# Filler rows, scatters, weight split and final gates of a mixture-of-experts block, rearranged around its drain

## The chip, the cores and the metric

The kernel runs on one core of a Trainium2 chip. The time is device microseconds of one execution. Engines are named as in the profile: PE (TensorE), DVE (VectorE), ACT (ScalarE), POOL (GpSimd) and SP (SyncE, which here only starts transfers). The kernel before has a median of 1559.16 us over three runs.

## The reference

The block takes 32 batches of 256 rows of 128 numbers. It is an attention layer followed by a mixture-of-experts feed-forward layer, each with a gate and a residual sum:

```python
mod = (_silu(L0_c) @ L0_wmod).reshape(L0_c.shape[0], 6, 1, -1)
sa, ca, ga, sb, cb, gb = (mod[:, k] for k in range(6))      # ga, gb are then kept at least 0.25 from zero
h = _layernorm(x) * (1 + ca) + sa
x = x + ga * attention(h)
h = _layernorm(x) * (1 + cb) + sb
x = x + gb * feed_forward(h)

# feed_forward: a router picks 2 of 8 experts for each row
logits = h @ router_w.T + router_b
topv, topi = top_k(logits, 2); gates = softmax(topv)
for e in range(8):
    w = sum(gates * (topi == e))
    y = (silu(h @ gate_w[e].T) * (h @ up_w[e].T)) @ down_w[e].T     # 128 -> 512 -> 128
    out += y * w
```

Everything is float32. The attention has 16 heads, each the difference of two softmaxes, and is not touched.

## The kernel before

The program has three stages. There is no scheduler: each engine's instructions stand in the order of the code, and engines wait for each other through semaphores.

**Attention, rounds.** `iterations` runs rounds i = -4 to 34. In one round eight batches are in work, each at another step: batch i (`b2`) has its scores, i-1 (`bC`) is normalised, i-2 (`bW`) gets its output product and residual sum, i-3 (`bR`) is routed. A round has 16 sub-steps `s`. The last three rounds, 32, 33 and 34, have no scores left; they are called the drain here. In them, for `bW`: DVE makes `on_tok` (L1308, s = 0), PE transposes it (L927), ACT copies it, PE multiplies by `wo` (L939), DVE makes `xtmp` (L1318), POOL adds it to `xres` (L1453), DVE takes statistics and inverse roots (L1267 to L1284), ACT writes the normalised row into `h2` (L1117). For `bR`: POOL scales and shifts `h2` in two passes (L1460 at s = 0, L1464 at s = 2), PE transposes it (L955) and multiplies by the router (L961), DVE picks the experts and counts (L1347 to L1402); `carry` holds the next free place of each expert, `idx` the place of each row. POOL then scatters the batch's four pieces of 128 rows into `rows_sorted` in DRAM (L1482, s = 12 to 15). `rows_sorted` has a region for each expert, and each row carries 128 numbers, the number of its place in `pair_out` and its gate.

**The way to the tiles.** An expert's rows seldom fill its last tile of 256, so filler rows (place number out of bounds, so never stored) are written behind each expert's end: `ffn_sp` reads the end from `endi` and starts one transfer per expert (L464 to L466), 256 rows each and 2304 behind the last. DVE makes tables of 72 tiles: each tile's expert (`tile_exp`) and first row (`tile_row`), L605 to L625. SP waits for the tables, the filler and all scatters, and then loads tile 0 (L482).

**Weights in two parts.** PE multiplies in a rounded float32 form, so a weight is used as a high part and a low part. `split_weights` (L389 to L402) does this on DVE for two experts in each of the three drain rounds and for two more behind the tables: for each half of an expert's weights a copy, a difference and a copy in place, so that `w_hi` holds the high and `kt`'s storage the low parts. For each tile ACT then copies the expert's high part into `w_now` (`bring_high`, L557) and DVE the low part (`bring_low`, L636).

**Feed-forward, tiles.** 72 tiles of 256 rows. For tile j PE transposes the rows of j+1 (L526), computes gate and up in two halves of three passes each (L515), and the down product of j-1 (L545). DVE splits the rows (L644, L646) and multiplies the halves (L654), ACT applies SiLU (L570) and scales the result (L579), POOL scatters it into `pair_out` (L680).

**Final sum.** 16 groups of two batches, in a ring of four slots. SP loads both experts' results (L498, two transfers) and the gates `gb`, repeated over the partitions, from DRAM (L501, one transfer); DVE adds the two results (L667) and multiplies by the gates (L670), POOL adds `xres` (L693), and a transfer started by ACT stores the group.

Of the kernel before, what the change touches and what calls it, by code (L numbers as in the profile page):

```python
# [5 lines left out]
F32 = mybir.dt.float32  # L6
F32R = mybir.dt.float32r
# [7 lines left out]
P = 128  # L15
# [30 lines left out]
LAST_PADS = FFN_TILES - ROUTED // FT + 1  # L46
# [53 lines left out]
def adaln_block(nc, x, w_qk, w_v, w_o, lambdas, rms_col, router_w, router_b, gate_w, up_w, down_w,  # L100
                c_t, w_mod, max_ones, ident, mask_q, before, iota, ramp, pair_no, tile_no, filler, out):
    ctx = ExitStack()
    with ctx:
# [50 lines left out]
        w_hi = sb("w_hi", [P, 2, NE * FF])  # L154
        wg, wu = (w_hi[:, k, :] for k in range(2))
# [146 lines left out]
        w_split = sem("w_split")  # L302
# [16 lines left out]
        fin_step = sem("fin_step")  # L319
        fin_done = sem("fin_done")  # L320
# [58 lines left out]
        lo_weights = kt[:].rearrange("p a t h k -> p (a t h k)").bitcast(F32)  # L379
        w_lo = lo_weights.rearrange("p (j k) -> p j k", j=2)  # L380
        wg_lo, wu_lo = (w_lo[:, k, :] for k in range(2))
# [8 lines left out]
        def split_weights(dve, c):  # L390

            V = nc.vector
            for w, lo in ((wg, wg_lo), (wu, wu_lo)):
                at = slice(c * FF, (c + 1) * FF)
                V.tensor_copy(lo[:, at].bitcast(F32R), w[:, at]).then_inc(w_split, 1)
                split_steps[0] += 1
                dve.wait_ge(w_split, split_steps[0])
                V.tensor_tensor(lo[:, at].bitcast(F32R), w[:, at], lo[:, at], ALU.subtract).then_inc(w_split, 1)  # L398
                split_steps[0] += 1
                dve.wait_ge(w_split, split_steps[0])  # L400
                V.tensor_copy(w[:, at].bitcast(F32R), w[:, at]).then_inc(w_split, 1)
                split_steps[0] += 1  # L402

        split_steps = [0]
        SPLIT_STEPS = 2 * 3 * NE
# [9 lines left out]
        fin_gb = (pair_view[:, FIN_RING * NF:FIN_RING * (NF + GROUP * DIM)]  # L415
                  .rearrange("p (a b c) -> p a b c", a=FIN_RING, b=GROUP))
# [41 lines left out]
        TABLE_STEPS = 17  # L458
# [1087 lines left out]
```

## Time and profile before

| | us |
|---|---|
| three runs | 1559.16, 1554.7, 1559.51 |
| the profiled execution | 1545.11 |
| its span, first to last instruction | 1543.4 |

Over the span PE is busy 1307.1 us (85%), DVE 1136.2, ACT 957.8 and POOL 875.8. The mean granted TensorE clock is 0.953 of full speed. The profile splits the span in 40 slices, and PE's digits are 9 nearly everywhere, except at the start, in four slices from the 27th on (the drain) and in the last two (the final sum). A busy share over the whole span mixes the stages, so the tables by stretch of time are read instead. The chain of work that ended last is followed back by the profile from the last instruction, each piece to what released it.

### The profile page before, as it was taken

Reading aid. Unit: us, or ns where it says so; the run is one execution under the profiler, and the core shown is the slowest. Engines: PE = TensorE matmul, PEld = TensorE weight load, DVE = VectorE, ACT = ScalarE, POOL = GpSimd, SP = SyncE. Lnnn points to the kernel's source line nnn. Section 1 sums busy time; section 2 is a strip of 40 time slices with the busy share of each in tenths; the row PEclk is TensorE's granted clock in tenths of the full one; section 3 lists DMA queues with packets and bytes.
Section 4 is the critical chain, followed back from the end, with each engine's and each line's share of the span. In section 5 each row is a group of like instructions: output and inputs, shape, how many; then the busy total and the mean of one; then the engine's idle time right before and its main releaser. Section 6 shows DMA issues by size and latency. Waiting matters only on the chain. (4 is left out here: it accounts for less than half of the span.)

```text
span 1543.4 us, 41532 instructions
## 1 busy us (share of the span) xinstructions
PE 1307.1 (85%) x13658; PEld 1068.2 (69%) x13785; DVE 1136.2 (74%) x2899; ACT 957.8 (62%) x2007; POOL 875.8 (57%) x1287
## 2 busy tenths in 40 slices
PE   1589999999999999999999999984179999999940
PEld 0366777767777777677776777663179999999940
DVE  4567888888888888888888888877745555555535
ACT  1166777777777777777777777763145555555520
POOL 2134667676777777677677677775313433444434
PEclk9999999999999999999999999996579999999985
DMA  6443345344434443444344434410121111111239
GB/s 218 119 110 84 107 119 127 91 113 121 124 93 121 114 124 91 121 120 118 91 127 113 120 92 117 118 39 22 46 71 52 53 51 52 52 55 52 54 103 283
DMA packets 178897, 154.20 MB, mean 100 GB/s; under 512 B 20851, under 2 KB 161401, under 8 KB 178340
## 3 DMA queue, kind: packets, MB, share of 16 engines
q1 hardware_dynamic: 161144, 124.63, 31.5%
q0 software_dynamic: 8704, 16.93, 3.6%
q10 hardware_dynamic: 8880, 10.49, 1.9%
q8 instruction: 93, 1.52, 0.4%
q14 instruction: 76, 0.62, 0.1%
HBM read 89.87 MB, written 63.14 MB: 99 GB/s over the span
## 5 line engine op out<-in xcount | busy, mean ns | idle before, releaser
L1021 ACT ACTIVATE probs<-p_exp 128x512 f32<-128x512 f32 x768 | 446.6, 602 | 176.1 <-PE p_exp L845 158.0
L1435 POOL TENSOR_SCALAR_AFFINE_SELECT probs<-probs 128x256 f32<-128x256 f32 (+1 forms) x768 | 365.5, 485 | 283.3 <-ACT probs L1021 275.5
L1199 DVE TENSOR_REDUCE mx<-p_max 128x2 f32<-128x512 f32 x512 | 351.2, 687 | 154.6 <-PE p_max L819 153.8
L680 POOL DMA_INDIRECT pair_out<-probs,v x144 | 141.5, 983 | 233.8 <-ACT probs L579 207.0
L817 PE MATMUL p_max<-kt,qt 96*128 96x256 bf16 x1024 | 198.6, 275 | 46.2 <-DVE mx L1199 24.4
L868 PE MATMUL p_out<-probs,v 128*32 128x256 f32 (+1 forms) x4096 | 220.8, 333 | 15.0 <-POOL probs L1435 8.7
L845 PE MATMUL p_exp<-qt,kt 100*128 100x256 bf16 x1024 | 196.0, 273 | 17.5 <-DMA qt<-max_parts 17.3
L1202 DVE TENSOR_REDUCE mx<-p_max 128x4 f32<-128x512 f32 x256 | 173.0, 676 | 1.6 <-PE p_max L828 1.6
L868 PEld LDWEIGHTS p_out<-probs,v 128*32 128x32 f32 x4096 | 112.3, 109 | 86.0 <-POOL probs L1435 25.1
L1482 POOL DMA_INDIRECT rows_sorted<-h,idx x128 | 136.7, 1068 | 51.1 <-issue 19.4
L817 PEld LDWEIGHTS p_max<-kt,qt 96*128 96x128 bf16 x1024 | 89.2, 101 | 90.1 <-DVE mx L1199 25.5
L570 ACT ACTIVATE ot<-p_exp 128x512 f32<-128x512 f32 x144 | 86.1, 598 | 90.9 <-PE p_exp L515 85.8
L819 PE MATMUL p_max<-mask,idb 128*128 128x256 bf16 x512 | 140.7, 275 | 0.0
L515 PE MATMUL p_exp<-rows_hi,w_now 128*128 128x256 f32 x576 | 140.0, 305 | 0.6 <-DVE w_now L636 0.6
L515 PE MATMUL p_max<-rows_hi,w_now 128*128 128x256 f32 x576 | 127.5, 283 | 0.0
L845 PEld LDWEIGHTS p_exp<-qt,kt 100*128 100x128 bf16 x1024 | 98.1, 98 | 37.5 <-DMA qt<-max_parts 23.7
L1011 ACT ACTIVATE ot<-p_out,out_scale 128x256 f32<-128x256 f32 x256 | 106.6, 472 | 0.0
L851 PE MATMUL p_exp<-qt,kt 100*128 100x128 bf16 x1024 | 99.4, 219 | 7.1
L1441 POOL TENSOR_TENSOR part_l<-rest,part_m 128x512 bf16<-128x512 f32 x64 | 74.4, 1162 | 52.0 <-ACT part_m L1037 52.0
L825 PE MATMUL p_max<-kt,qt 96*128 96x128 bf16 x1024 | 100.8, 221 | 2.0 <-DVE mx L1199 1.1
L515 PEld LDWEIGHTS p_exp<-rows_hi,w_now 128*128 128x128 f32 x576 | 100.0, 191 | 1.0 <-issue 1.0
L851 PEld LDWEIGHTS p_exp<-qt,kt 100*128 100x128 bf16 x1024 | 79.4, 98 | 30.5 <-issue 0.6
(166 smaller groups left out, 2770.6 us busy)
## 6 DMA issues: line engine op xcount, KB each, us to landing
qt<-q_parts SPq DMA_DIRECT2D x64, 384.0 KB
q_parts<-part_h SPq DMA_DIRECT2D x96, 128.0 KB, 2.0
kt<-k_parts SPq DMA_DIRECT2D x128, 96.0 KB
v<-rows_sorted SPq DMA_DIRECT2D x72, 130.0 KB, 2.2
q_parts<-part_m SPq DMA_DIRECT2D x64, 128.0 KB, 2.0
kt<-k_parts SPq DMA_DIRECT2D x128, 64.0 KB
qt<-pair_out SPq DMA_DIRECT2D x32, 256.0 KB, 5.2
mods<-mod_rows SPq DMA_DIRECT2D x32, 192.0 KB, 3.9
```

The costliest lines, as they stand in the source:

```text
L515: m = nc.tensor.matmul(to[:, f * FT:(f + 1) * FT], w_now[:, par, w, kind, (f0 + f) * P:(f0 + f + 1) * P], rows[:, par, :], start=(k == 0), ...
L680: nc.gpsimd.indirect_dma_start(pair_out, bass.IndirectOffsetOnAxis(rows_in[:, j.slot, t, DIM:DIM + 1].bitcast(U32), 0), rows_out[:, j.slot ...
L817: nc.tensor.matmul(p_max[:, bank, t * SEQ:(t + 1) * SEQ], qt[0:QK_ROWS, slot, h8, P:SEQ], kt[0:QK_ROWS, slot, t, h8, :], start=(t == 0), s ...
L819: m = nc.tensor.matmul(p_max[:, bank, :].rearrange("p (t k) -> p t k", t=2)[:, :, P:SEQ], idb[:], mask4[:, 0:2, :], start=False, stop=True)
L845: m = nc.tensor.matmul(p_exp[:, bank, t * SEQ:(t + 1) * SEQ], kt[0:ALL_ROWS, slot, t, h8, 0:P], qt[0:ALL_ROWS, slot, h8, :], start=True, s ...
L851: m = nc.tensor.matmul(p_exp[:, bank, c:c + P], kt[0:ALL_ROWS, slot, t, h8 - 1 + hh, P:SEQ], qt[0:ALL_ROWS, slot, h8 - 1 + hh, P:SEQ], sta ...
L868: m = nc.tensor.matmul(p_out[32 * j:32 * j + 32, g % 2, SEQ - n:SEQ], v[:, b.par, tile, 2 * g + j // 2, :], src, start=(tile == 0), stop=( ...
L1021: nc.scalar.activation(probs[:, g % 2, k, :], p_exp[:, k, :], ACT.Exp, scale=SCALE).then_inc(exp_done.sem, 1)
L1199: m = V.reduce_max(mx[:, w, 1, :, h8:h8 + 1].rearrange("p t o -> p (t o)"), p_max[:, bank, :].rearrange("p (t k) -> p t k", t=2), AX.X, ne ...
L1202: m = V.reduce_max(mx[:, w, 0, :, h8 - 1:h8 + 1], p_max[:, bank, :].rearrange("p (t h k) -> p t h k", t=2, h=2), AX.X, negate=True)
L1435: G.affine_select(out=blocks, in_=blocks, compare_op=ALU.is_ge, fill=zero, base=0, pattern=[[0, 2 if k < 2 else 4], [1, P]], channel_multi ...
L1482: G.indirect_dma_start(rows_sorted, bass.IndirectOffsetOnAxis(idx[:, bR.par, k:k + 1].bitcast(U32), 0), h2[:, bR.par, k // NT, k % NT, :], ...
```

## The change

1. *Filler.* `endi` is now copied one batch earlier, when the last batch but one (30) has been routed, and 512 rows are written behind each expert's end as it stands then (`AHEAD`), which covers what the last batch can add. The 2048 rows behind the eight regions have a fixed place and are written at the start, by a transfer that ACT issues. POOL's first scatter of the last batch waits for all nine.
2. *Scatters.* Batch 30's four scatters move from s = 12 to 15 of round 33 to s = 3 to 6 of round 34.
3. *Weights.* `split_weights` is gone. The weights stay whole in `w_all`; ACT's copy into `w_now` rounds them as before, and DVE makes the low part of a tile's expert as `w_all` less that copy, for which it waits for the copy.
4. *Tables.* Tiles behind the last expert's are told by an eighth comparison, since they lie in the fixed filler.
5. *Final gates.* The repeated gates come from PE: a column of the identity, repeated, times `mrow`, into four PSUM banks. The transfer from `mod_rows` is gone.

```diff
-LAST_PADS = FFN_TILES - ROUTED // FT + 1
+LAST_PADS = FFN_TILES - ROUTED // FT
+AHEAD = (SEQ + FT) // P
+FILLS = NE + 1
...
-        def split_weights(dve, c):
...
-                V.tensor_copy(lo[:, at].bitcast(F32R), w[:, at]).then_inc(w_split, 1)
...
-                V.tensor_tensor(lo[:, at].bitcast(F32R), w[:, at], lo[:, at], ALU.subtract).then_inc(w_split, 1)
...
-                V.tensor_copy(w[:, at].bitcast(F32R), w[:, at]).then_inc(w_split, 1)
...
-        fin_gb = (pair_view[:, FIN_RING * NF:FIN_RING * (NF + GROUP * DIM)]
-                  .rearrange("p (a b c) -> p a b c", a=FIN_RING, b=GROUP))
+        fin_gb = (p_exp[:, 0, :], p_exp[:, 1, :], p_max[:, 0, :], p_max[:, 1, :])
...
-                start = sp.value_load(endi[0:1, e:e + 1], min_val=0, max_val=SORTED_ROWS - LAST_PADS * FT)
-                pads = (FT if e < NE - 1 else LAST_PADS * FT) // P
-                sp.dma_start(rows_sorted[bass.ds(start, pads * P), :].rearrange("(m p) r -> p m r", p=P),
-                             fill[:].unsqueeze(1).to_broadcast([P, pads, RW])).then_inc(filled, 16)
+                start = sp.value_load(endi[0:1, e:e + 1], min_val=0, max_val=NE * REGION - AHEAD * P)
+                sp.dma_start(rows_sorted[bass.ds(start, AHEAD * P), :].rearrange("(m p) r -> p m r", p=P),
+                             fill[:].unsqueeze(1).to_broadcast([P, AHEAD, RW])).then_inc(filled, 16)
...
-                sp.dma_start(fin_gb[:, g.slot, :, :],
-                             mod_rows[bass.ds(g.n * GROUP, GROUP), 3 * DIM:4 * DIM].unsqueeze(0)
-                             .to_broadcast([P, GROUP, DIM])).then_inc(fin_loaded[g.slot], 16)
...
-            pe.wait_ge(w_split, SPLIT_STEPS)
...
+            pe.wait_ge(hid_ready, 2 * FFN_TILES)
+            for g in range(NB // GROUP):
+                if g >= FIN_RING:
+                    pe.wait_ge(fin_step, 2 * (g - FIN_RING) + 2)
+                for j in range(GROUP):
+                    b = g * GROUP + j
+                    m = nc.tensor.matmul(fin_gb[g % FIN_RING][:, j * DIM:(j + 1) * DIM],
+                                         idf[0:NB, b:b + 1].to_broadcast([NB, P]), mrow[:, 3, :], start=True, stop=True)
+                m.then_inc(gb_ps, 1)
...
-                    V.tensor_copy(w_now[:, j.c % 2, 1, :, :], w_lo[:, :, bass.ds(w0, FF)]).then_inc(low_here, 1)
+                    t_wait(dve, high_here, j)
+                    V.tensor_tensor(w_now[:, j.c % 2, 1, :, :], w_all[:, :, bass.ds(w0, FF)],
+                                    w_now[:, j.c % 2, 0, :, :].bitcast(F32), ALU.subtract).then_inc(low_here, 1)
...
+                dve.wait_ge(gb_ps, g.n + 1)
                 fo = fin_out[:, g.slot, :].rearrange("p (b t c) -> p b t c", b=GROUP, c=DIM)
-                V.tensor_tensor(fo, fo, fin_gb[:, g.slot, :, :].unsqueeze(2).to_broadcast([P, GROUP, NT, DIM]), ALU.mult).then_inc(fin_step, 1)
+                gb = fin_gb[g.slot][:, 0:GROUP * DIM].rearrange("p (b c) -> p b c", b=GROUP)
+                V.tensor_tensor(fo, fo, gb.unsqueeze(2).to_broadcast([P, GROUP, NT, DIM]), ALU.mult).then_inc(fin_step, 1)
...
             act.wait_ge(setup_v, SETUP_DONE)
+            act.dma_start(rows_sorted[NE * REGION:SORTED_ROWS, :].rearrange("(m p) r -> p m r", p=P),
+                          fill[:].unsqueeze(1).to_broadcast([P, LAST_PADS * FT // P, RW])).then_inc(filled, 16)
...
-                    for c in range(2):
-                        split_weights(dve, 2 * (i.c - NB) + c)
...
                             V.tensor_copy(idx[:, bR.par, :], posf[:]).then_inc(route.sem, 1)
+                            if bR.c == NB - 2:
+                                V.tensor_copy(endi[:], carry[:]).then_inc(tables, 1)
...
+            def scatter(b, k):
+                if k == 0:
+                    wait(pool, route, b, ROUTE_ROWS)
+                    wait(pool, h2_copied, b)
+                    if b.c == NB - 1:
+                        pool.wait_ge(filled, 16 * FILLS)
...
-                    if s in (12, 13, 14, 15) and active(bR):
...
+                    if s in (12, 13, 14, 15) and active(bR) and bR.c != NB - 2:
+                        scatter(bR, s - 12)
+                    if s in (3, 4, 5, 6) and bR.c == NB - 1:
+                        scatter(bR.plus(-1), s - 3)
```

How the order of the instructions moves is shown at three places. The first is DVE at the start of round 33, before the change: the roots of round 32 (`rstd`, `neg_mr`), the first split group (one half of one expert), of which three more alike follow, and then `on_tok`.

```order
L1282 SCALAR_TENSOR_TENSOR rstd<-nt,root 128x36
L1284 SCALAR_TENSOR_TENSOR neg_mr<-mvs,rstd 128x4
L395 CAST kt<-w_hi 128x512
L398 TENSOR_TENSOR kt<-w_hi,kt 128x512
L401 CAST w_hi<-w_hi 128x512
```

From the same list, the end of the fourth group and what follows it: `on_tok` stands behind all twelve.

```order
L398 TENSOR_TENSOR kt<-w_hi,kt 128x512
L401 CAST w_hi<-w_hi 128x512
L1308 TENSOR_TENSOR on_tok<-o,rstd 128x512
L1318 TENSOR_TENSOR xtmp<-p_mix,mods 128x256
L1242 BN_STATS stats<-xres 128x6 x2
```

The same place after the change, with that program's own line numbers (L1289 is `on_tok`, L1299 `xtmp`).

```order
L1270 SCALAR_TENSOR_TENSOR rstd<-nt,root 128x36
L1272 SCALAR_TENSOR_TENSOR neg_mr<-mvs,rstd 128x4
L1289 TENSOR_TENSOR on_tok<-o,rstd 128x512
L1299 TENSOR_TENSOR xtmp<-p_mix,mods 128x256
L1230 BN_STATS stats<-xres 128x6 x2
```

Twelve instructions between the roots and `on_tok` are gone; the same holds for rounds 32 and 34, and behind the tables.

The second place is POOL from the end of round 32 to the first stores of the tiles, before the change; each row of four DMAs is one batch's scatters (29, 30, 31), `h<-h,mods` are the two passes.

```order
L1482 DMA rows_sorted<-h,idx 69888x130 x4
L1460 TENSOR_TENSOR h<-h,mods 128x2x128
L1464 TENSOR_TENSOR h<-h,mods 128x2x128
L1453 TENSOR_TENSOR xres<-xres,xtmp 128x256
L1482 DMA rows_sorted<-h,idx 69888x130 x4
L1460 TENSOR_TENSOR h<-h,mods 128x2x128
L1464 TENSOR_TENSOR h<-h,mods 128x2x128
L1482 DMA rows_sorted<-h,idx 69888x130 x4
L680 DMA pair_out<-probs,v 16384x128 x12
```

And after it, where the eight DMAs are batch 30's and batch 31's scatters.

```order
L1428 DMA rows_sorted<-h,idx 69632x130 x4
L1453 TENSOR_TENSOR h<-h,mods 128x2x128
L1457 TENSOR_TENSOR h<-h,mods 128x2x128
L1446 TENSOR_TENSOR xres<-xres,xtmp 128x256
L1453 TENSOR_TENSOR h<-h,mods 128x2x128
L1457 TENSOR_TENSOR h<-h,mods 128x2x128
L1428 DMA rows_sorted<-h,idx 69632x130 x8
L666 DMA pair_out<-probs,v 16384x128 x12
```

Batch 30's scatters have gone behind the passes over batch 31's `h`; batch 29's still stand ahead of those over batch 30's.

The third place is SP from the last tile's load (`v<-rows_sorted`) to the loads of the first two groups of the final sum, before the change.

```order
L482 DMA v<-rows_sorted 128x2x130
L498 DMA qt<-pair_out 128x4x128 x2
L501 DMA probs<-mod_rows 128x2x128
L498 DMA qt<-pair_out 128x4x128 x2
L501 DMA probs<-mod_rows 128x2x128
```

And after it; the last row is the eight loads of the first four groups.

```order
L461 TENSOR_LOAD tile_row
L461 ISA x2
L462 ISA
L462 DMA v<-rows_sorted 128x2x130
L478 DMA qt<-pair_out 128x4x128 x8
```

Of three transfers a group two are left.

## Rows read from the trace of the kernel before

**Rows 1.** Windows: length; busy (x) PE, PEld, DVE, ACT, POOL; clock; DMA share; GB/s.

```profile
1050.00:1130.00 80.00, 19.49 (x130) 13.93 (x129) 50.46 (x161) 15.17 (x38) 29.65 (x32) 0.54 0.17 48
1130.00:1480.00 350.00, 349.37 (x2988) 349.00 (x2988) 202.31 (x357) 203.44 (x354) 137.56 (x140) 0.99 0.19 51
1480.00:1543.40 63.40, 4.41 (x37) 4.01 (x35) 30.86 (x33) 1.85 (x5) 24.49 (x21) 0.58 0.83 232
```

**Rows 2.** Timeline of PE in the drain: start, duration, what, [idle before <-releaser].

```profile
1063.72 1.09 PE L927 MATMUL p_mix<-idf,on_tok 128*128 128x128 f32 x4 [2.92 <-DVE on_tok L1308]
...
1089.24 0.69 PE L955 MATMUL p_mix<-idf,h 128*128 128x128 f32 x2 [0.52 <-DVE xtmp L1318]
```

**Rows 3.** Timeline of DVE in the drain.

```profile
1054.31 0.42 DVE L395 CAST kt<-w_hi 128x512 fp32r<-128x512 f32 x1
...
1076.59 0.42 DVE L395 CAST kt<-w_hi 128x512 fp32r<-128x512 f32 x1
...
1083.51 1.17 DVE L1308 TENSOR_TENSOR on_tok<-o,rstd 128x512 f32<-128x512 f32 x1
...
1113.63 0.23 DVE L625 SCALAR_TENSOR_TENSOR tile_row<-tileno,qt 128x72 int32<-128x72 f32 x1
```

**Rows 4.** Timeline of POOL in the drain.

```profile
1076.74 1.15 POOL L1482 DMA_INDIRECT rows_sorted<-h,idx  x1 [3.40 <-DVE idx L1402]
...
1082.15 1.15 POOL L1460 TENSOR_TENSOR h<-h,mods 128x256 f32<-128x256 f32 x1
1083.38 0.75 POOL L1464 TENSOR_TENSOR h<-h,mods 128x256 f32<-128x256 f32 x1
...
1112.89 0.96 POOL L1482 DMA_INDIRECT rows_sorted<-h,idx  x1 [0.30 <-issue]
```

**Rows 5.** Timeline of ACT in round 33.

```profile
1095.56 0.88 ACT L1117 ACTIVATE h<-xres,neg_mr,rstd 128x128 f32<-128x128 f32 x2 [1.55 <-DVE neg_mr L1284]
```

**Rows 6.** The chain that ended last, in order of time: start, duration, what.

```profile
1101.17 0.70 POOL h L1460
...
1102.84 0.67 PE p_mix L955 x2
...
1108.08 0.15 DVE idx L1402
...
1109.39 0.41 SPq L466
...
1117.46 7.54 DMA rows_sorted<-fill
...
1125.78 2.17 DMA v<-rows_sorted
```

**Rows 7.** DMA issues: what, queue, count, size of each, median us to landing.

```profile
pair_out<-probs,v POOLq DMA_INDIRECT x144, 2.3
...
rows_sorted<-fill SPq DMA_DIRECT2D x7, 130.0 KB, 2.3
```

**Rows 8.** Windows, columns as in rows 1: the filler's transfer, and the final sum.

```profile
1122.00:1123.00 1.00, 0.00 (x0) 0.00 (x0) 0.00 (x0) 0.98 (x2) 0.00 (x0) 0.50 1.21 253
1530.00:1535.00 5.00, 0.00 (x0) 0.00 (x0) 3.81 (x5) 0.00 (x0) 2.52 (x2) 0.50 1.16 338
```

**Rows 9.** Timeline of DVE in the final sum: the first and the last group's add.

```profile
1495.90 0.69 DVE L667 TENSOR_TENSOR probs<-qt 128x512 f32<-128x512 f32 x1 [12.76 <-DMA probs<-mod_rows]
...
1536.05 1.55 DVE L667 TENSOR_TENSOR probs<-qt 128x512 f32<-128x512 f32 x1 [0.43 <-DMA probs<-mod_rows]
```

**Rows 10.** Timeline of one DVE instruction of the setup, and of a tile.

```profile
26.45 1.23 DVE L1188 TENSOR_TENSOR probs<-probs,idf 128x1024 f32<-128x1024 f32 x1
...
1308.72 1.05 ACT L557 CAST w_now<-w_hi 128x1024 fp32r x1 [0.20 <-PE p_max L515]
1309.46 0.69 DVE L636 CAST w_now<-kt 128x1024 fp32r x1 [0.16 <-issue]
...
1311.69 0.37 PE L515 MATMUL p_exp<-rows_hi,w_now 128*128 128x256 f32 x1
```

More of the change, by code:

```diff
@@ L153, in adaln_block @@
         mrow = sb("mrow", [NB, 4, DIM])
-        w_hi = sb("w_hi", [P, 2, NE * FF])
-        wg, wu = (w_hi[:, k, :] for k in range(2))
+        w_all = sb("w_all", [P, 2, NE * FF])
         wd = sb("wd", [P, NE * FF])
@@ L556, in bring_high @@
                     w0 = act.value_load(tile_exp[0:1, bass.ds(j.n, 1)], min_val=0, max_val=(NE - 1) * FF)
-                    nc.scalar.copy(w_now[:, j.c % 2, 0, :, :], w_hi[:, :, bass.ds(w0, FF)]).then_inc(high_here, 1)
-            act.wait_ge(w_split, SPLIT_STEPS)
+                    nc.scalar.copy(w_now[:, j.c % 2, 0, :, :], w_all[:, :, bass.ds(w0, FF)]).then_inc(high_here, 1)
+            act.wait_ge(ffn_w_loaded, 48)
             act.wait_ge(tables, TABLE_STEPS)
@@ L595, in ffn_vector @@
             V = nc.vector
-            count = [0]
+            count = [1]
             def step(ins):
@@ L603, in ffn_vector @@
             dve.wait_ge(route.sem, ROUTE_STEPS * NB)
-            step(V.tensor_copy(endi[:], carry[:]))
             step(V.tensor_tensor(ends[:], carry[:], posm_ramp[:], ALU.subtract))
@@ L612, in ffn_vector @@
             step(V.tensor_scalar(jump[:], first[:], -float(FT), float(REGION), ALU.mult, ALU.add))
[L613 removed]
+            for e in range(1, NE):
                 step(V.tensor_tensor(first[:, e:e + 1], first[:, e:e + 1], first[:, e - 1:e], ALU.add))
[L616 removed]
+            ge = table_view[:, 0:FFN_TILES * NE].rearrange("p (j e) -> p j e", e=NE)
             sums = table_view[:, FFN_TILES * NE:FFN_TILES * (NE + 1)]
             dve.wait_ge(pv_done.sem, PAIRS * NB)
[L619 to L620 removed]
+            step(V.tensor_tensor(ge, tileno[:].unsqueeze(2).to_broadcast([P, FFN_TILES, NE]),
+                                 first[:].unsqueeze(1).to_broadcast([P, FFN_TILES, NE]), ALU.is_ge))
             step(V.reduce_sum(sums, ge, AX.X))
[L622 to L623 removed]
+            V.tensor_scalar(tile_exp[:], sums, float(FF), float((NE - 1) * FF), ALU.mult, ALU.min)
+            step(V.tensor_tensor(ge, ge, jump[:].unsqueeze(1).to_broadcast([P, FFN_TILES, NE]), ALU.mult))
             step(V.reduce_sum(sums, ge, AX.X))
@@ L626, in ffn_vector @@
             assert count[0] == TABLE_STEPS, count
-            for c in range(2 * TAIL, NE):
-                split_weights(dve, c)
-            assert split_steps[0] == SPLIT_STEPS
+            dve.wait_ge(ffn_w_loaded, 48)
             def bring_low(j):
@@ L661, in final @@
             def final(g):
-                dve.wait_ge(fin_loaded[g.slot], 48 * (g.turn + 1))
+                dve.wait_ge(fin_loaded[g.slot], 32 * (g.turn + 1))
                 if not g.static:
```

43 lines of the change are left out of this document (8 added, 35 removed).

## The prediction

> **What bounds the kernel now.** I read the windows by stage first. In the feed-forward tiles PE is busy for 349.37 of 350.00 us at a granted clock of 0.99 [rows 1]: nothing off PE's path is worth anything there, and whatever makes PE wait is paid 72 times. Between attention and the tiles (1050 to 1130 us, the drain) no engine is full: PE is busy 19.49 of 80 us and the DMA share is 0.17 [rows 1]. That is a chain of single steps, and a step taken out of it is worth its full length. In the final sum PE is all but idle and the DMA share is 0.83 over the stretch [rows 1] and 1.16 in the middle of it [rows 8]: the transfers look like the limit. The change touches all three.
>
> Which steps of the drain count I read from the timelines of PE, DVE and POOL beside each other and from the chain of waits. The drain has three rounds (32, 33, 34). In round 32 PE has ended its last `p_out` work and sits idle for 2.92 us, until 1063.72, for `on_tok` [rows 2], while DVE splits weights from 1054.31 on [rows 3]. In round 33 the split runs from 1076.59 to 1083.51 [rows 3]; POOL meanwhile issues four scatters, from 1076.74 to 1082.15, and then makes its two passes over `h`, the second until 1084.13 [rows 4]. In round 34 `h` is ready for POOL at 1096.44 [rows 5], but POOL comes to it at 1101.17, behind four more scatters [rows 6]. After the last `idx` (1108.23) come eight issues of filler from 1109.39 on; the last starts at 1117.46 and takes 7.54 us to land, and only then does the first tile's load start, at 1125.78 [rows 6].
>
> **The change part by part.** All times are on the clock of the profiled execution.
>
> *Split out of round 32.* Twelve instructions leave DVE, but PE has other work until 1063.72 - 2.92 = 1060.80 [rows 2], so 2.9 us come back. If POOL's masks and scatters, which release that other work, also ran quicker without the split beside them, it could be up to 2 us more; I take none of it.
>
> *Split out of round 33.* DVE's branch would bring PE's transposes of `h` (1089.24 [rows 2]) forward by 6.9 us [rows 3]. But they also need POOL's second pass, which as it is ends at 1084.13 [rows 4]; PE would start some 0.15 later, at 1084.3: 4.9 us. So POOL is late next. Its own pace: a scatter beside the split took 1.15 us, the very last one, after the split group beside it began but among nothing else of POOL's, 0.96 [rows 4]; if all four come down to 0.96, 0.8 us more. I take a little over half, 5.4 us. The Trainium skill, page "SBUF — State Buffer", section "Who interferes with whom", says that VectorE's copies and casts in a two-port mode lock GpSimd out of the shared ports, through which it writes its descriptors. By that rule in full the round gives 5.7 us back, without it 4.9; the trace has both durations, but a split runs beside the short one too, so it bears the rule out only in part.
>
> *Scatters moved behind the passes over `h`.* In round 34 POOL can start on `h` at 1096.5 [rows 5] in place of 1101.17 [rows 6], 4.7 us, less some 0.2 for the `endi` cast that now stands ahead of the roots on DVE: 4.5 us. The four scatters are not gone: they stand between these passes and the last batch's scatters. The next `idx` comes 5.4 us after PE's transposes start (1102.84 to 1108.23 [rows 6]); four scatters of 0.96 us with gaps of 0.30 [rows 4] and 0.7 us ahead of them are 5.7. Nearly hidden, and the filler (below) is later anyway.
> So far 2.9 + 5.4 + 4.5 = 12.8 us: the last `idx` at 1095.4.
>
> *Filler ahead.* The eight issues now follow the last batch but one. Its `idx` comes 5.4 us after its transposes, at 1094.65 (1089.24 + 5.4), less 2.9 + 5.4 = 8.3 us: 1086.35. The first issue follows `idx` by 1.15 us as now (1108.23 to 1109.39, `endi` cast included), so 1087.5; the eighth 8.1 us later (1109.39 to 1117.46 [rows 6]): 1095.6. It carries 260 KB. The 130 KB ones landed in 2.3 us [rows 7], the 1170 KB one in 7.54 [rows 6]; on that line 3.0. All eight are 2.13 MB in 8.1 us, 263 GB/s, and the big one ran at 253 GB/s with the engines full [rows 8], so they queue a little: I take 3.8 us, landed at 1099.4 (bounds 1098 to 1103). This is a new wait. The last batch's first scatter stands behind it on POOL, behind that the other three, and SP waits for all of them before it loads tile 0. From 1099.4: 0.3 us, 3 x 1.27 to the start of the fourth scatter, 2.3 us to land (as the tiles' scatters do [rows 7]): 1105.8. SP then takes 0.8 us, as between the filler's landing (1125.02) and the load (1125.78) [rows 6]: the load starts at 1106.6 in place of 1125.78, 19.2 us earlier. The tables need 1113.86 - 1108.23 = 5.6 us from `idx` [rows 3, 6], now some 0.4 more (one more step, 576 elements for 504): 1101.4, in time. The split's last group behind them was hidden under the filler already.
>
> *Low part made per tile.* DVE's copy of 128x1024 takes 0.69 us; a TENSOR_TENSOR of 128x1024 took 1.23 [rows 10]. Before the first tile this is on the path: 0.5 us. In the loop it must also wait for ACT's high copy, which ends at 1308.72 + 1.05 = 1309.77 [rows 10]; so the low part runs from 1309.9 to 1311.1, and PE takes up the next tile's weights at 1311.69 [rows 10]. A margin of 0.5 us: cost 0. Here the change could lose most.
>
> *Final sum.* Group to group it takes (1536.05 - 1495.90) / 15 = 2.68 us [rows 9]. A group moves 512 KB in, 256 KB out and 128 KB of gates (896 KB). With the engines at 1.16 [rows 8] I let time follow bytes: 2.68 x 128 / 896 = 0.38 us a group, 5.7 us over 15, and 0.3 for the issue that goes ahead of the first group's data: 6.0 us. Bounds: 0, if the ring of four slots sets the pace and not the bytes; 9, if the landing gets quicker on top. DVE's multiply now reads PSUM, which no row shows in this stage; I bound it by the add of its shape, 0.69 alone and 1.55 beside POOL's add [rows 9], at 0.69. PE's gate products are due long before they are read.
>
> *Start.* ACT issues 1.06 MB of filler behind 6 MB of weights. At 253 GB/s [rows 8] that is 4.2 us of the engines, at worst all on the path, at best none. I take 0.3 us, near the lower end, since nothing waits for this filler before the drain. The Trainium skill, "DMA: Bandwidth & Descriptors", section "Issuing engines are not separate DMA queues", speaks against the change here: DMAs of ACT, SP and GpSimd run on the same 16 engines and interleave. If the first batches' loads stood behind it in full, the sum would be 20.5 in place of 24.4 us; the trace of before has no such transfer.
>
> **Sum**: 19.2 - 0.5 + 6.0 - 0.3 = 24.4 us. The profiled execution would go from 1545.11 us (span 1543.4) to 1520.7. The median of the runs, 1559.16, lies 14 us above the profiled execution, and nothing in the trace says why; taken off the median: 1534.8 us.
>
> **Rivals.**
> (a) The final sum gives nothing: its pace is the ring. From the fifth group on a slot's loads wait for POOL's sum in that slot; SP's issues, landing, DVE's two steps and POOL's add are 4 x 2.68 us around. For: DVE's add grows from 0.69 to 1.55 us beside POOL's add [rows 9], and both stay. Against: the share of 1.16 [rows 8], and that one of the issues in this very ring goes. Gain 18.4: 1540.8. Chance 0.14.
> (b) The filler lands late. If the transfers and POOL's scatters jam the engines so that the last lands as late as the 1170 KB one did, 7.5 us after its issue [rows 6], 3.7 us go, and with them the 0.5 of POOL's own pace and part of the final sum. Gain 19 or less: 1541. Chance 0.10.
> (c) More than forecast: round 32 gives 2 more, the filler isn't late at all (3 more), the final sum 9 in place of 6. Gain 32: 1527. Chance 0.12.
> (d) Slower than before: the low part makes PE wait in every tile. A TENSOR_TENSOR of two SBUF inputs grew from 0.69 to 1.55 us beside POOL [rows 9]; were the low part stretched alike, 1.23 x 1.55 / 0.69 = 2.8 us, PE would wait 2.8 - 1.23 - 0.5 = 1.0 us a tile, 74 us over 72 tiles: 1609. It decides from 24.4 / 72 = 0.34 us of wait a tile on, a low part of 2.1 us. Against: in the tiles POOL has scatters and no adds, and between its two of a tile and the next two lies the time of the low part. The SBUF page's same section lets two SBUF inputs contend only with a GpSimd instruction that reads SBUF. Chance 0.04, a quarter of it small enough to end within 0.3%.
> (e) The change does nothing: the drain ends in another wait as long, such as tile 0 on its tables and on ACT's first high copy. The tables are there at 1101.4 and the copy takes 1.05 us [rows 10], long before the rows: too early to decide. Chance 0.02.
>
> **How the numbers follow.** Forecast 0.58, (a) 0.14, (b) 0.10, (c) 0.12, (d) 0.04, (e) 0.02. The range takes in (a), (b) and most of (c), and goes a little further down than their sum because the base is loose: the runs before spread from 1554.7 to 1559.51 with the profiled one at 1545.11. 1522 to 1545. About 0.3% (4.7 us) is what a measurement of this kernel can tell from no change. Faster 0.94 (forecast, (a), (b), (c)), same 0.03, slower 0.03.
>
> **What would show it.** Right: no cast into `kt` in the drain; PE's transposes of `on_tok` straight behind its `p_out` work; POOL's passes over `h` straight behind ACT; the last batch's first scatter released by a filler DMA; tile 0's load 19 us earlier; the tiles at the pace of before with DVE's low part at 1.23; groups of 2.3 us in the final sum. Wrong: PE waiting for `w_now` in the loop, groups still at 2.7 us, or the last batch's first scatter more than 5 us behind `idx`.

## The result, and the profile after

The changed kernel took 1537.6 us (median of four runs, 1527.53 to 1540.76) against 1556.93 for the kernel before (median of four, 1553.02 to 1559.51): a ratio of 0.9864, 95% interval 0.9836 to 0.9893, which is 21.2 us less (17 to 26); the two medians as they stand are 19.3 us apart. The forecast was 1534.8 us, 24.4 less than the 1559.16 us that the kernel before had then; one more run has since moved that median to 1556.93, so the time came a little closer to the forecast than the gain did.

The two profiled executions are 1543.4 us of span before and 1538.6 after, only 4.8 apart. That is no contradiction. The attention stage, which the change leaves alone, is not equally long in every execution: PE's last `p_out` work ended at 1060.80 in the profile before and at 1077.17 in the one after, and over the ten profiles of this study, all with the same code for the attention rounds, it ended anywhere from 1060.57 to 1077.17. So I set all clocks to zero at the end of PE's last `p_out` work and compare from there. On that clock the rest takes 482.60 us before (1543.4 - 1060.80) and 461.43 after: 21.2 us, which fits the timed ratio. The forecast column splits the prediction's 19.2 us up to the load of tile 0 into the pieces that it names and a rest.

| piece, from trace to trace | before | after | gained | forecast |
|---|---|---|---|---|
| round 32: last `p_out` to the end of its roots (`neg_mr`) | 15.87 | 12.90 | 2.97 | 2.9 |
| round 33: to PE's transposes of batch 30's `h` | 12.57 | 6.92 | 5.65 | 5.4 |
| round 34: to those of batch 31's `h` | 13.60 | 8.90 | 4.70 | 4.5 |
| from there to the load of tile 0 | 22.94 | 21.69 | 1.25 | 6.4 |
| to the first product of tile 0 | 5.32 | 6.10 | -0.78 | -0.5 |
| the tiles, to the last down product | 354.23 | 354.57 | -0.34 | 0 |
| final sum, to POOL's last add | 54.43 | 46.80 | 7.63 | 6.0 |
| last store | 3.64 | 3.55 | 0.09 | 0 |

PE in the drain of the changed kernel (timeline: start, duration, what, idle before and its releaser). L913 transposes `on_tok`, L941 transposes `h`.

```profile
1075.66 1.51 PE L854 MATMUL p_out<-probs,v 128*32 128x256 f32 x16 [3.68 <-POOL probs L1418]
1077.10 1.12 PE L913 MATMUL p_mix<-idf,on_tok 128*128 128x128 f32 x4
...
1096.99 0.66 PE L941 MATMUL p_mix<-idf,h 128*128 128x128 f32 x2 [2.25 <-POOL h L1457]
...
1105.89 0.66 PE L941 MATMUL p_mix<-idf,h 128*128 128x128 f32 x2 [4.46 <-POOL h L1457]
```

The 2.92 us of idle time before the `on_tok` transposes [rows 2] are gone, and PE now waits for POOL in round 33, as forecast. POOL, from the end of round 33:

```profile
1104.30 0.68 POOL L1453 TENSOR_TENSOR h<-h,mods 128x256 f32<-128x256 f32 x1 [6.78 <-ACT h L1105]
1105.06 0.68 POOL L1457 TENSOR_TENSOR h<-h,mods 128x256 f32<-128x256 f32 x1
1105.89 1.01 POOL L1428 DMA_INDIRECT rows_sorted<-h,idx  x1 [0.15 <-issue]
...
1109.74 0.96 POOL L1428 DMA_INDIRECT rows_sorted<-h,idx  x1 [0.30 <-issue]
1120.65 0.96 POOL L1428 DMA_INDIRECT rows_sorted<-h,idx  x1 [9.95 <-DMA rows_sorted<-fill]
```

The passes over `h` start right behind ACT's row, in place of behind four scatters [rows 4 to 6]. But the last batch's first scatter then waits 9.95 us for the filler. The chain of waits of the same stretch, in order of time:

```profile
1102.28 0.18 DVE endi L1385
...
1103.41 0.41 SPq L446
...
1112.56 7.20 DMA rows_sorted<-fill
...
1124.44 2.27 DMA rows_sorted<-h,idx
...
1127.58 2.31 DMA v<-rows_sorted
```

The path now runs from batch 30's `endi` through the eight transfers to the last batch's scatters. Round 34, with the gain of 4.7 us in it, lies beside this path and not on it. The engines behind the filler (windows: length, busy time of PE, PEld, DVE, ACT, POOL, clock, DMA share, GB/s):

```profile
1108.00:1110.00 2.00, 0.10 (x1) 0.00 (x0) 1.35 (x10) 0.48 (x2) 1.39 (x3) 0.50 1.24 164
1110.00:1112.00 2.00, 0.25 (x4) 0.19 (x4) 1.48 (x13) 0.00 (x0) 0.70 (x1) 0.50 1.30 178
1112.00:1114.00 2.00, 0.00 (x0) 0.00 (x0) 1.69 (x10) 0.00 (x0) 0.00 (x0) 0.50 1.19 176
```

They are full at 164 to 178 GB/s, where the one long transfer before moved 253 at the same share [rows 8]. Neither rate is steady. The first four microseconds of the eight transfers moved more, at a lower share:

```profile
1104.00:1106.00 2.00, 0.11 (x1) 0.14 (x2) 0.00 (x0) 0.22 (x1) 1.47 (x3) 0.50 0.66 200
1106.00:1108.00 2.00, 1.45 (x6) 1.07 (x6) 0.00 (x0) 0.68 (x2) 1.70 (x2) 0.50 0.84 237
```

And the long transfer of the kernel before, in the three microseconds ahead of the one in [rows 8]:

```profile
1119.00:1120.00 1.00, 0.00 (x0) 0.00 (x0) 0.97 (x2) 0.00 (x0) 0.00 (x0) 0.50 0.95 295
1120.00:1121.00 1.00, 0.00 (x0) 0.00 (x0) 0.08 (x1) 0.00 (x0) 0.00 (x0) 0.50 1.03 287
1121.00:1122.00 1.00, 0.00 (x0) 0.00 (x0) 0.00 (x0) 0.44 (x1) 0.00 (x0) 0.50 1.20 189
```

With the 253 of [rows 8] its four microseconds average 256 GB/s.

In the tiles, PE stays busy for 349.37 of 350 us, to the hundredth what it was [rows 1]; the low part takes 1.23 us and ends 0.57 us before PE's first product of the next tile:

```profile
1134.00:1484.00 350.00, 349.37 (x2995) 349.16 (x2995) 238.96 (x355) 204.11 (x355) 138.46 (x140) 1.00 0.19 50
```

```profile
1311.64 1.05 ACT L543 CAST w_now<-w_all 128x1024 fp32r x1 [0.19 <-issue]
1312.81 1.23 DVE L619 TENSOR_TENSOR w_now<-w_all,w_now 128x1024 fp32r<-128x1024 f32 x1 [0.60 <-ACT w_now L543]
...
1314.61 0.37 PE L491 MATMUL p_exp<-rows_hi,w_now 128*128 128x256 f32 x1
```

In the final sum DVE's first and last add, against those of [rows 9]:

```profile
1497.40 0.69 DVE L651 TENSOR_TENSOR probs<-qt 128x512 f32<-128x512 f32 x1 [11.35 <-DMA qt<-pair_out]
...
1532.02 0.68 DVE L651 TENSOR_TENSOR probs<-qt 128x512 f32<-128x512 f32 x1
```

(1532.02 - 1497.40) / 15 = 2.31 us a group, in place of 2.68, with the engines as full as before (DVE's multiply, which now reads PSUM, takes 0.69 us as it did):

```profile
1523.00:1528.00 5.00, 1.50 (x6) 0.93 (x4) 3.73 (x5) 0.00 (x0) 3.42 (x3) 0.50 1.16 335
```

### The profile page after: what moved, and what is told of

It reads as the page before. It is cut to its first block and busy times, and to the rows that moved or that the text cites. A ratio compares the mean times of both kernels' runs of the same rounds, so it can differ in the third digit from the quotient of the medians.

```text
span 1538.6 us, 41590 instructions
## 1 busy us (share of the span) xinstructions
PE 1335.9 (87%) x13722; PEld 1082.5 (70%) x13849; DVE 1130.0 (73%) x2852; ACT 961.9 (63%) x2007; POOL 877.8 (57%) x1287
## 5 line engine op out<-in xcount | busy, mean ns | idle before, releaser
L619 DVE TENSOR_TENSOR w_now<-w_all,w_now 128x1024 fp32r<-128x1024 f32 x72 | 88.2, 1225 | 31.4 <-issue 24.5
```

## The experiments

Each changes one thing in the changed kernel, except fill_contiguous_earlier, which joins two of them, and the last, which starts from the kernel before. The code is cut to its main lines. Times of runs are to be compared only with the kernel before in the same runs: 1545.92 us (median of seven) for the first four experiments, 1554.82 (median of thirteen) for the others. Times named +x are microseconds behind the end of PE's last `p_out` work of the same trace. In the changed kernel batch 30's `idx` is at +25.20, the last batch's first scatter at +43.48 and tile 0's load at +50.41.

Two of the runs below, gates_dead_load and low_margin, have the drain of the changed kernel untouched, and so show how much it differs between executions. The last filler transfer in them:

```profile
1107.86 7.10 DMA rows_sorted<-fill
```

```profile
1102.93 6.70 DMA rows_sorted<-fill
```

From batch 30's `idx` to its landing it is 16.8 us in the first (1114.96 - 1098.17), 16.4 in the second (1109.63 - 1093.24) and 17.4 in the changed kernel; tile 0's load is at +49.89, +49.04 and +50.41. A difference of about 1 us in the drain, seen in one trace, is no effect.

### scatter_back: is the scatters' new place worth anything?

```diff
-                    if s in (12, 13, 14, 15) and active(bR) and bR.c != NB - 2:
+                    if s in (12, 13, 14, 15) and active(bR):
                         scatter(bR, s - 12)
-                    if s in (3, 4, 5, 6) and bR.c == NB - 1:
-                        scatter(bR.plus(-1), s - 3)
```

> The changed kernel with batch 30's four scatters back at s = 12 to 15 of round 33, ahead of POOL's passes over h; all else as changed. Theory (the filler's transfers set the end of the drain): from the idx of batch 30 to the first scatter of batch 31 stays 18.3 us (1102.37 to 1120.65 after), POOL's passes over h come 4.7 us later and PE's L941 with them, and nothing of it reaches the load of tile 0: time within 1 us of the changed kernel. Rival 1 (the move is worth its 4.5 us, as forecast): 4 to 5 us longer. Rival 2 (batch 30's scatters in the midst of the filler slow it): the filler lands more than 1 us earlier or later than 17.4 us after idx of batch 30.

1524.78 us (ratio to the kernel before in the same runs 0.9851, 0.981 to 0.9891), no different from the changed kernel's 0.9864. POOL:

```profile
1094.16 0.96 POOL L1428 DMA_INDIRECT rows_sorted<-h,idx  x1 [0.31 <-issue]
1095.15 0.69 POOL L1453 TENSOR_TENSOR h<-h,mods 128x256 f32<-128x256 f32 x1
...
1106.53 1.33 POOL L1428 DMA_INDIRECT rows_sorted<-h,idx  x1 [9.93 <-DMA rows_sorted<-fill]
```

The passes over `h` start behind the scatters again, PE's transposes at +32.13 in place of +28.72, and yet the last batch's first scatter waits 9.93 us for the filler all the same. It starts at +41.92 and tile 0's load at +49.23. From batch 30's `idx` (+24.86) to that scatter it is 17.1 us, and to the filler's landing 16.2 (1105.63 - 1089.47), against 17.4 in the changed kernel's trace but 16.4 in the quickest other trace of the same drain. So rival 2 is not shown: what is left for it is 0.2 us. Rival 1 is out. The 4.7 us of round 34 are real and worth nothing.

### fill_contiguous: why is the filler slow?

```diff
-        fill = sb("fill", [P, RW])
+        fill = sb("fill", [P, AHEAD, RW])
...
-                sp.dma_start(rows_sorted[bass.ds(start, AHEAD * P), :].rearrange("(m p) r -> p m r", p=P),
-                             fill[:].unsqueeze(1).to_broadcast([P, AHEAD, RW])).then_inc(filled, 16)
+                sp.dma_start(rows_sorted[bass.ds(start, AHEAD * P), :].rearrange("(p m) r -> p (m r)", p=P),
+                             fill[:].rearrange("p m r -> p (m r)")).then_inc(filled, 16)
...
```

The lines left out load `fill` with the filler row repeated, and let ACT's transfer at the start read one of its copies.

> The changed kernel with the eight filler transfers of the drain written as one run of 4 rows (2080 bytes) per partition from a wider tile, in place of four runs of 520 bytes; same bytes, same rows. Theory A (the transfers are slow by their many short pieces): the last filler lands some 3 us after its issue in place of 7.2, issues are not held back (8.1 us in place of 9.2), tile 0's load 5 us earlier. Theory B (bytes written, or a fixed cost of each of the eight transfers, whatever the pieces): the last lands 6 to 7.5 us after its issue and the time stays within 1 us.

1521.21 us (0.9825, 0.9784 to 0.9867; this overlaps the changed kernel's interval, so the trace has to decide). The same bytes, in pieces four times as long. The chain of waits, and the windows of the fullest stretch:

```profile
1095.23 3.80 DMA rows_sorted<-fill
...
1107.03 2.26 DMA v<-rows_sorted
```

```profile
1092.00:1094.00 2.00, 0.13 (x1) 0.03 (x1) 1.35 (x10) 0.48 (x2) 1.39 (x3) 0.50 0.78 288
1094.00:1096.00 2.00, 0.25 (x4) 0.19 (x4) 1.45 (x13) 0.00 (x0) 0.74 (x1) 0.50 0.86 291
```

The last transfer lands in 3.80 us, the engines are no longer full and move 291 GB/s, and tile 0's load is at +45.83: 4.6 us earlier than in the changed kernel's trace, 3.2 than in the quickest other one of its drain. From the last `p_out` work to the end it is 458.30 us in place of 461.43. Theory A holds against theory B: bytes and number of transfers are the same, so it was the layout in many short pieces. With the length of a piece the order of the rows in DRAM and the reading of `fill` change too; these were not tried apart.

### fill_two_queues: the issues or the engines behind them?

```diff
-            for e in range(NE):
+            for e in range(0, NE, 2):
...
+                    if s == 0 and bR.static and bR.c == NB - 1:
+                        act.wait_ge(tables, 1)
+                        for e in range(1, NE, 2):
+                            start = act.value_load(endi[0:1, e:e + 1], min_val=0, max_val=NE * REGION - AHEAD * P)
+                            act.dma_start(rows_sorted[bass.ds(start, AHEAD * P), :].rearrange("(m p) r -> p m r", p=P),
+                                          fill[:].unsqueeze(1).to_broadcast([P, AHEAD, RW])).then_inc(filled, 16)
```

> The changed kernel with four of the eight filler transfers started by ACT at the start of round 34 and four by SP. If the issues on SP set the pace (1.15 to 1.3 us each), the last lands about 4 us earlier against idx of batch 30 (13.4 in place of 17.4 us). If the 16 engines behind both queues do, as the share of 1.2 to 1.3 says, it lands at 16.5 to 17.5 us still.

One run, 1528.87 us. The last of the eight is issued 6.8 us behind batch 30's `idx` in place of 10.2, and takes 2.2 us longer:

```profile
1097.83 9.36 DMA rows_sorted<-fill
```

It lands at +41.37 (1107.19 - 1065.82), 16.2 us behind batch 30's `idx`; in the changed kernel that was 17.4 (1119.76 - 1102.37), and 16.4 to 16.8 in the two other traces of its drain. Of 3.4 us of issues saved at most 1.2 come back, and 0.2 against the quickest of the others: the engines behind the queues set it.

### fill_earlier: is starting earlier a cure?

```diff
-AHEAD = (SEQ + FT) // P
+AHEAD = (2 * SEQ + FT) // P
...
-                            if bR.c == NB - 2:
+                            if bR.c == NB - 3:
                                 V.tensor_copy(endi[:], carry[:]).then_inc(tables, 1)
...
-                    if b.c == NB - 1:
+                    if b.c == NB - 2:
                         pool.wait_ge(filled, 16 * FILLS)
```

> The changed kernel with endi copied after batch 29 and 768 rows of filler behind each expert (half as many bytes again); batch 30's scatters wait for it too. At the 158 GB/s of the changed kernel the 3.2 MB take 20 us, from some 2 us behind the idx of batch 29; they land at 1111 to 1113 on the clock of the changed kernel's trace, eight scatters follow, the last starts at about 1122 in place of 1124.44: 2 us faster. If the rate is worse with longer transfers, no gain or a loss; if it is better (the 1170 KB transfer of before ran at 253 GB/s), the filler is no longer waited for by batch 31 and the gain is 7 to 9 us.

1521.55 us (0.9841, 0.9794 to 0.9888, again no different from the changed kernel by the runs alone). Batch 30's scatters wait for the filler now, and the last batch's stand straight behind them:

```profile
1088.46 0.68 POOL L1457 TENSOR_TENSOR h<-h,mods 128x256 f32<-128x256 f32 x1
1094.61 1.01 POOL L1428 DMA_INDIRECT rows_sorted<-h,idx  x1 [5.47 <-DVE h L1381]
...
1103.52 0.96 POOL L1428 DMA_INDIRECT rows_sorted<-h,idx  x1 [0.30 <-issue]
```

The releaser named, an instruction of DVE of that moment, can't be what the scatter waited for: batch 30's rows were long routed, and the only other wait in front of it is the one for the filler. The load is at +46.16, 4.25 us earlier than in the changed kernel (2.9 than in the quickest other trace of its drain), where I expected 2 at the changed kernel's rate. From the last `p_out` work to the end it is 458.73 us, 2.7 less. Half as many bytes again, and still a gain.

### fill_contiguous_earlier: both cures together

```diff
-        fill = sb("fill", [P, RW])
+        fill = sb("fill", [P, 3, RW])
...
+                sp.dma_start(rows_sorted[bass.ds(start, AHEAD * P), :].rearrange("(q p m) r -> p q (m r)", p=P, m=3),
+                             fill[:].rearrange("p m r -> p (m r)").unsqueeze(1).to_broadcast([P, AHEAD // 3, 3 * RW])).then_inc(filled, 16)
...
```

With it go the three edits of fill_earlier, and the same two lines left out as in fill_contiguous.

> Filler one batch earlier (768 rows an expert) and in long pieces (1560 bytes). If long pieces are what made the filler fast and starting it earlier what took it off the path, both add: no engine waits for the filler, batch 30's scatters start right behind POOL's passes over h, 28.7 us after PE's last p_out work as in the changed kernel, batch 31's at 34.9 us behind its idx, tile 0's load at 42.0 (changed kernel 50.4, fill_contiguous 45.8, fill_earlier 46.2). From PE's last p_out work to the end 454.5 us (before 482.6, changed 461.4). If the two cures are for the same wait and don't add, the load stays at 45.8.

1520.32 us against 1554.82 for the kernel before in the same runs: 0.9788 (0.9758 to 0.9819). The interval lies wholly below that of the changed kernel, so this version is faster than the kernel before and than the changed one. POOL:

```profile
1094.27 0.68 POOL L1457 TENSOR_TENSOR h<-h,mods 128x256 f32<-128x256 f32 x1
1095.11 1.01 POOL L1428 DMA_INDIRECT rows_sorted<-h,idx  x1 [0.15 <-issue]
...
1098.94 0.95 POOL L1428 DMA_INDIRECT rows_sorted<-h,idx  x1 [0.30 <-issue]
1101.34 0.95 POOL L1428 DMA_INDIRECT rows_sorted<-h,idx  x1 [1.44 <-issue]
```

Nothing waits for the filler. Batch 30's scatters start at +28.70, the last batch's 0.85 us behind its `idx` (+34.08), and the load is at +41.98. From the last `p_out` work to the end it is 453.19 us, 8.2 less than in the changed kernel (expected 454.5). `idx` of the last batch is now what comes last in front of its scatters, so here the scatters' new place should pay; this version with the scatters put back was not run.

### gates_dead_load: what sets the pace of the final sum?

```diff
             def final(g):
                 act.wait_ge(fin_done, g.n + 1)
+                act.dma_start(pair_view[:, FIN_RING * NF:FIN_RING * (NF + GROUP * DIM)]
+                              .rearrange("p (a b c) -> p a b c", a=FIN_RING, b=GROUP)[:, g.slot, :, :],
+                              mod_rows[bass.ds(g.n * GROUP, GROUP), 3 * DIM:4 * DIM].unsqueeze(0)
+                              .to_broadcast([P, GROUP, DIM])).then_inc(fin_stored[g.slot], 16)
...
```

The lines left out make the waits for `fin_stored` count this transfer too, so DVE's add into a slot also waits for its dead load.

> The changed kernel with the transfer of the gates from mod_rows kept, started by ACT ahead of each group's store and read by nobody, so that its bytes are moved again while SP still issues two transfers a group. If the bytes set the pace of the final sum, groups take 2.6 to 2.7 us again (changed 2.31) and the stage 5 us more; if the issues on SP or the ring of four slots do, groups stay at 2.3 us.

One run, 1542.9 us. Groups take 2.68 us again, the very pace of the kernel before, and the stage up to POOL's last add 52.06 in place of 46.80: 5.3 us. (In the six other traces with the new final sum the stage takes 46.7 to 48.5 us, so at least 3.6.)

```profile
1510.00:1515.00 5.00, 2.44 (x8) 1.85 (x8) 2.89 (x4) 0.00 (x0) 2.52 (x2) 0.50 1.16 336
1515.00:1520.00 5.00, 2.44 (x8) 1.85 (x8) 3.95 (x5) 0.00 (x0) 2.46 (x2) 0.50 1.17 326
```

The same 326 to 336 GB/s with 896 KB a group as with 768: bytes set the pace, not SP's issues. The ring as the limit by itself (rival (a)) is out too, since the same ring of four goes round in 2.31 us a group with fewer bytes. The run doesn't part the bytes wholly from a longer turn of the ring: in 3 of the last 12 groups the profile puts DVE's wait down to the store and not to the load.

### low_margin: how much room did the low part have?

```diff
                     t_wait(dve, high_here, j)
+                    V.tensor_tensor(on_tok[:].rearrange("p t k -> p (t k)"), o[:].rearrange("p a k -> p (a k)"),
+                                    o[:].rearrange("p a k -> p (a k)"), ALU.add)
+                    V.tensor_tensor(on2[:, 0:1].rearrange("p a h t d -> p (a h t d)"), o[:].rearrange("p a k -> p (a k)"),
+                                    o[:].rearrange("p a k -> p (a k)"), ALU.add)
                     V.tensor_tensor(w_now[:, j.c % 2, 1, :, :], w_all[:, :, bass.ds(w0, FF)],
```

> The changed kernel with two adds of 128x512 (0.69 us each, results unused) ahead of DVE's low part in every tile. The trace of the changed kernel leaves 0.57 us from the end of the low part (1314.04) to PE's first product of the next tile (1314.61), and 0.75 in the next tile. If that margin is right, PE waits 1.4 - 0.6 = 0.8 us a tile and the tiles take 50 to 65 us more. If PE had more slack than that (low parts are read only in the third pass of a product), less than 20 us; if the low part were on the path already, 100 us.

One run, 1579.63 us; the tiles took 401.24 us in place of 354.57, 46.7 more or 0.65 a tile. Who waited for whom in the tiles (us in total, times, longest):

```profile
PE p_exp L491 <- DVE w_now L623: 29.9, 72, 2.3
...
PEld p_exp L491 <- ACT ot L556: 24.5, 39, 0.8
```

The two adds hold DVE for 1.2 to 1.3 us a tile (the second starts 0.6 us behind the first), less the 0.65 that the tiles lengthen: a margin of about 0.6 us, as the trace of the changed kernel shows. I had reckoned with 1.4 for the pair and so expected a few us too much. The margin is real and small: a low part 0.6 us longer would have begun to cost, at the place that rival (d) named.

### split_by_tile_only: one part of the change alone

Kernel before, with the split stage and its waits taken out and the low part made as in the changed kernel:

```diff
-                    for c in range(2):
-                        split_weights(dve, 2 * (i.c - NB) + c)
...
-                    V.tensor_copy(w_now[:, j.c % 2, 1, :, :], w_lo[:, :, bass.ds(w0, FF)]).then_inc(low_here, 1)
+                    t_wait(dve, high_here, j)
+                    V.tensor_tensor(w_now[:, j.c % 2, 1, :, :], w_hi[:, :, bass.ds(w0, FF)],
+                                    w_now[:, j.c % 2, 0, :, :].bitcast(F32), ALU.subtract).then_inc(low_here, 1)
```

> The kernel before with one part of the change alone: no split stage, low parts made tile by tile. By the trace of the changed kernel: 3.0 us from round 32 and 5.6 from round 33, nothing from round 34 (POOL's scatters stand ahead of the passes over h as before) nor behind the tables, 0.6 lost before tile 0: 7.5 to 8 us off the 482.6 us from PE's last p_out work to the end, so 475. If the split had been hidden under POOL's scatters in round 33 as well, 2.5 us; if POOL's own quickening counts in round 34 too, 9 us.

1543.41 us (0.993, 0.9906 to 0.9954). From the last `p_out` work to the end it is 473.80 us, 8.8 less than before; 0.7 of them lie in the final sum, which this version leaves alone, so 8.1 belong to it. Rounds 32 and 33 take 12.90 and 6.92 us, as in the changed kernel. POOL in round 34:

```profile
1095.25 1.01 POOL L1478 DMA_INDIRECT rows_sorted<-h,idx  x1 [5.69 <-DVE idx L1398]
1096.56 0.96 POOL L1478 DMA_INDIRECT rows_sorted<-h,idx  x1 [0.30 <-issue]
...
1099.09 0.96 POOL L1478 DMA_INDIRECT rows_sorted<-h,idx  x1 [0.30 <-issue]
1100.07 0.70 POOL L1456 TENSOR_TENSOR h<-h,mods 128x256 f32<-128x256 f32 x1
```

Without the split groups on DVE beside them, the scatters of this round take 0.96 to 1.01 us where they took 1.14 to 1.22, and the step from one PE transpose of `h` to the next shrinks by 0.95 us (13.60 to 12.65), with POOL's order unchanged. It does not hold for every scatter without a copy beside it. The first one of round 33 starts beside DVE's `on_tok`, a TENSOR_TENSOR of two SBUF inputs:

```profile
1082.02 0.69 DVE L1304 TENSOR_TENSOR on_tok<-o,rstd 128x512 f32<-128x512 f32 x1
1082.18 1.42 POOL L1478 DMA_INDIRECT rows_sorted<-h,idx  x1 [3.40 <-DVE idx L1398]
```

It takes 1.42 us, more than any scatter beside the split; the other three of that round take 0.96. So POOL's quickening counts in round 34, as the last variant of the expectation had it; its 9 us are met only with the 0.7 of the final sum.

## Why the prediction was right, and where it was off

The forecast held: faster, 21.2 us against 24.4, and the time 2.8 us above the forecast. The mechanisms were the ones named, but one term was off by a fifth of the whole, and that the total came so near is in part luck, as said below.

*Split out of rounds 32 and 33.* Right to 0.3 us (2.97 and 5.65 against 2.9 and 5.4), and shown alone by split_by_tile_only. POOL was late next in round 33, as the prediction said. Its price for POOL's own quickening was not right in kind. From the first of the four scatters of that round to the first pass over `h` it was 5.24 us (1090.15 to 1095.39) in place of 5.41 (1076.74 to 1082.15), since the first scatter, beside `on_tok`, grew to 1.42: 0.2 us gained, where 0.8 was reckoned with 0.96 for each. Another 0.5 us came from the two passes themselves, 1.45 us in place of 1.98 with the split no longer beside the first. The Trainium skill, page "SBUF — State Buffer", section "Who interferes with whom", says that VectorE's copies and casts in a two-port mode lock GpSimd out of the shared ports; taken in full the prediction made 5.7 us of it. The round gave 5.65, but not by the scatters, so that agreement is luck; the scatters of round 34 (split_by_tile_only) are where the traces bear the rule out. One reading was wrong as well: the last scatter of the kernel before (0.96 us, ended at 1113.85 [rows 4]) had no split beside it, since the last groups start only then:

```profile
1113.90 0.43 DVE L395 CAST kt<-w_hi 128x512 fp32r<-128x512 f32 x1
```

*Scatters behind the passes over `h`.* The size was right (4.70 against 4.5); on the path it had none, and the prediction's own figures say so: the last `idx` at 1095.4 stands 4.0 us in front of the filler's landing at 1099.4, and the 19.2 us of the sum are worked out along the filler, from batch 30's `idx`, with no 4.5 in them. The prediction said that the filler is later anyway, but not that the move was then worth nothing; scatter_back shows it.

*Filler ahead: the term that was mis-sized.* The prediction had the eighth transfer issued 8.1 us behind the first and landed 3.8 us later. It was issued 9.15 us behind it (1103.41 to 1112.56) and landed 7.20 us later, 17.4 us behind batch 30's `idx` against 13.05 forecast (16.4 and 16.8 in the two other traces of this drain). From the landing to the first scatter it was 0.9 us in place of 0.3. That is rival (b), nearly to its number (7.5). The line drawn through 130 KB in 2.3 us and 1170 KB in 7.54 was drawn through seven transfers beside which the engines were about half busy (DMA share 0.41 to 0.64 from 1110 to 1118 us), and one that stood alone at the end; eight of 260 KB in a row are another case. The sum set 263 GB/s against the 253 of [rows 8] and took a queue of 0.8 us for it. At 253 that is even ample, since 2.13 MB take 8.4 us at that rate against 8.1 of issues. What failed is the 253 itself, one microsecond of one transfer: from 1108 on the eight moved 164 to 178 GB/s, and none of the rows that the sum used has that rate. fill_two_queues shows that the engines and not the issues held it, fill_contiguous that the layout in short pieces did.

*Low part.* The duration was exact (1.23 us). The way to the first tile cost 0.78 in place of 0.5, because the load itself took 2.31 us in place of 2.17 and the low part came 0.1 later behind its wait. In the tiles the margin was 0.57 against 0.5, and low_margin measures it from the other side. Rival (d) did not come about: the low part took 1.23 us in the tiles, not 2.8.

*Final sum.* By bytes the groups should quicken by 0.38 us each; they did by 0.37 (5.5 us over 15), and gates_dead_load gives those back with the bytes put back. The rest of the 7.63 is the first group, whose add starts 4.17 us behind SP's first issue in place of 5.59 (1.4 us), and the last, from whose add to POOL's end it is 3.03 us in place of 3.71 (0.7). I had 0.3 for both. The stage takes 46.7 to 48.5 us in seven traces with the new final sum, so most of the 1.6 us above the forecast may be the luck of this one.

*Start.* No cost of ACT's filler is to be seen: PE's first score product starts at 82.38 us in place of 82.47, and at 81.50 to 82.62 in all ten traces, the two without this transfer at 82.47 and 81.58. It is issued at 29.13 us, behind the weights. The 16 us by which the attention stage varies arise later.

The two errors, -5.15 us at the filler and +1.63 in the final sum, and the small ones (+0.3 together) make up the 3.2 us between forecast and result. Without the surplus of the final sum the gain would have been 19.5 us, near the 19 of rival (b). The forecast was right in direction and size; for the path to tile 0 the rival was.

## What to carry to other kernels

When a transfer is moved forward off a path, put its own rate into the sum before its new slack, and take that rate from as many bytes in the same layout as will be in flight, not from one microsecond of one transfer (253 GB/s there, 164 to 178 here). Where the transfer ends last all the same, gains of the path beside it (here 4.7 us of round 34) are worth nothing. Several filler or clearing transfers should be laid out in runs as long as the data allow; here four rows a piece in place of one was worth as much as starting a whole batch earlier (4.6 and 4.25 us, a trace each). And where executions vary in a stage that the change doesn't touch, set the clocks to zero behind it; that made 21 us visible between two profiles whose spans differ by 5.

## What the runs showed of the hardware

Eight transfers of 512 pieces of 520 bytes each moved 164 to 178 GB/s with the DMA share at 1.19 to 1.30; the same bytes in 128 pieces of 2080 moved 288 to 291 at a share of 0.78 to 0.86. One single transfer of 2304 pieces of 520 bytes had moved 256 GB/s over four microseconds (295, 287, 189, 253 one by one), and the eight began at 200 and 237 before they fell. Whether the fall comes with the number of transfers in flight or with the time for which short pieces are written was not tried and stays open. A scatter of 128 rows took 0.96 to 1.01 us on POOL with no larger DVE instruction beside it, 1.14 to 1.22 beside the split groups (one of eight 0.95), and 1.42 beside DVE's `on_tok`. The mean round of the attention stage also differs between executions of equal code, with the granted TensorE clock from 260 to 860 us at 1.00 in the kernel before and fill_contiguous, which were quick, and at 0.99 in the changed kernel, which was slow; whether the clock is the cause or goes along with it stays open.
